# Inverse softmax sums of six of eight head pairs made inside a block's last pair; chain of the last two pairs beside the out-products

## The reference

```python
x = x + layernorm(attn(layernorm(x)))       # attn ends in: softmax(scores) @ v, heads joined, @ wo
x = x + layernorm(ffn(layernorm(x)))        # router, top 2 of 16 experts, one shared expert
```

## Time and profile before

| what | us |
|---|---|
| median of 3 runs | 1311.3 (1304.27 to 1312.95) |
| profiled execution, its own time | 1306.9 |
| its span, first to last instruction | 1305.1 |
| mean granted TensorE clock | 0.968 of full speed |
| PE busy | 1154.6 (88%) |
| DVE busy | 832.9 (64%) |
| ACT busy | 795.2 (61%) |
| POOL busy | 732.5 (56%) |

### The profile page before, as it was taken

The page is one execution under the profiler, slowest core; times in us unless marked ns, Lnnn a source line. Parts: engine busy times, 40 slices in busy tenths (PEclk is TensorE's granted clock), DMA queues, the critical chain, the costliest instruction groups (busy, mean ns, idle before and its releaser), DMA issues. The chain is left out here.

```text
span 1305.1 us, 19781 instructions
## 1 busy us (share of the span) xinstructions
PE 1154.6 (88%) x6552; PEld 549.4 (42%) x6563; DVE 832.9 (64%) x2104; ACT 795.2 (61%) x1237; POOL 732.5 (56%) x444
## 2 busy tenths in 40 slices
PE   3997999999998999999999979999999999788820
PEld 2643545344443533444443523333433334466710
DVE  6556786666667766565756786676666625745637
ACT  3633762766665466766666367777787783356632
POOL 0046541465564076766666248888888894435545
PEclk9988999999999999999999999999999999989975
DMA  9135300110011010000011001000000000367754
GB/s 286 34 87 131 91 1 1 49 33 17 21 45 34 6 44 17 17 17 17 17 33 32 11 13 57 26 13 13 25 25 25 13 13 17 71 130 211 187 135 141
DMA packets 63031, 70.25 MB, mean 54 GB/s; under 512 B 10080, under 2 KB 52448, under 8 KB 62816
## 3 DMA queue, kind: packets, MB, share of 16 engines
q1 hardware_dynamic: 56656, 56.26, 15.8%
q0 software_dynamic: 4864, 10.51, 3.7%
q10 hardware_dynamic: 1424, 2.38, 0.7%
HBM read 37.51 MB, written 14.83 MB: 40 GB/s over the span
## 5 line engine op out<-in xcount | busy, mean ns | idle before, releaser
L567 POOL TENSOR_TENSOR D<-D,B 128x1024 f32<-128x1024 f32 (+3 forms) x256 | 513.4, 2006 | 140.5 <-ACT B L759 120.2
L759 ACT ACTIVATE B<-ps 128x1024 f32<-128x1024 f32 (+1 forms) x320 | 285.2, 892 | 206.6 <-PE ps L1699 121.0
L1124 DVE TENSOR_REDUCE mxp<-ps 128x1 f32<-128x512 f32 x384 | 260.4, 688 | 177.2 <-PE ps L1673 175.1
L646 ACT ACTIVATE ps<-D 128x1024 f32<-128x1024 f32 (+3 forms) x327 | 288.3, 883 | 24.1 <-DVE D L1142 14.4
L1720 PE MATMUL ps<-B,kv 128*64 128x512 f32 (+3 forms) x1280 | 278.9, 545 | 0.3
L1699 PE MATMUL ps<-A,KTh 128*128 128x512 f16 (+3 forms) x768 | 209.0, 354 | 4.0 <-ACT ps L646 3.9
L560 POOL TENSOR_TENSOR D<-B 128x1024 f32<-128x1024 f32 (+1 forms) x32 | 70.8, 2213 | 209.1 <-ACT B L759 209.1
L1126 DVE CUSTOM_DVE_ANT_0 ps<-ps,c 128x128 f32<-128x128 f32 (+3 forms) x256 | 126.6, 496 | 76.9 <-PE ps L1673 73.4
L1673 PE MATMUL ps<-KTh,A 128*128 128x512 f16 (+3 forms) x384 | 134.4, 357 | 10.4 <-DVE mxp L1124 8.7
L1699 PE MATMUL ps<-A,KTl 128*128 128x512 f16 (+3 forms) x384 | 135.8, 354 | 0.0
L1720 PEld LDWEIGHTS ps<-B,kv 128*64 128x64 f32 x1280 | 73.6, 135 | 113.7 <-issue 97.0
(11 more groups left out here) (273 smaller groups left out, 1785.3 us busy)
## 6 DMA issues: line engine op xcount, KB each, us to landing
results<-B SPq DMA_DIRECT2D x64, 128.0 KB
xnTl<-in_L_ffn_experts_gate_up SPq DMA_DIRECT2D x16, 256.0 KB, 2.8
A<-in_L_attn_wq SPq DMA_DIRECT2D x4, 768.0 KB, 20.6
B<-in_L_attn_x SPq DMA_DIRECT2D x5, 512.0 KB, 5.6
D<-in_L_attn_wo SPq DMA_DIRECT2D x2, 1024.0 KB, 20.3
A<-C SPq DMA_DIRECT2D x16, 128.0 KB, 2.3
A<-C SPq DMA_DIRECT2D x32, 64.0 KB, 2.0
A<-stg SPq DMA_DIRECT2D x16, 128.0 KB, 2.3
```

The source lines that it names most:

```text
L567: nc.gpsimd.tensor_tensor(acc[:, :, c0:], acc[:, :, c0:], Pr[:, kt % P_RING, :, c0:], ALU.add).then_inc(sum_done, 1)
L646: return nc.scalar.activation(dst, src, ACT.Copy, scale=scale)
L759: nc.scalar.activation(Pr[:, kt % P_RING, :, c0:], ps[:, 2 * (kt % ST_RING):2 * (kt % ST_RING) + 2, c0:], ACT.Exp, scale=SM_SCALE).then_in ...
L1124: V.tensor_reduce(most, rough, AX.X, ALU.max).then_inc(mx_free, 1)
```

## The change

The denominators of pairs 0 to 5 are made inside the block's last pair (pair 7), at the slots of `EARLY`; those of pairs 6 and 7 (`LATE_PAIRS = 2`) after it. `Lp` is set to 1.0 at the kernel's start, so that the early reciprocal reads a number for the pairs that are not there yet; both chains work on all 16 heads. The terms, the turn and the copy are thus made twice in each block, with their own buffers (`early_terms` in `scr_r`, `early_rows` in `c32`). Inverse spreads go to banks 2 and 3 instead of 7 and 6.

At the block's end PE spreads pairs 0 and 1 at once, keeps four idle matmuls (before: 18, in block 3: 29), makes the products of row tiles 0 and 1 for pairs 0 to 5, then those of tile 2, among which the late chain's matmuls stand, then pairs 6 and 7 of tiles 0 to 2, and last the eight products of tile 3. DVE's layer-norm steps of the four tiles are staggered, with the moments of tiles 0 and 1 ahead of the first `with_input`.

```diff
+EARLY = [(3, 6), (18, 21), (24, 28), (6, 10)]
+LATE_PAIRS = 2
...
         def inv_bank(n):
-            return BK_O if n % 2 else BK_M
+            return 2 + n % 2
...
+                    if p == NP - 1 and kt == EARLY[qc][1] // 3:
+                        act.wait_ge(e_turned_ready, qc + 1)
+                        copy(early_rows[0:3 * H, :], ps[0:3 * H, BK_M, :]).then_inc(e_inv_ready, 1)
...
+                    if p == NP - 1 and slot == EARLY[qc][0] + 1:
+                        dve.wait_ge(e_den_ready, qc + 1)
+                        link(V.reciprocal(rL[:, :, :].rearrange("p h j -> p (h j)"), ps[:, BK_M, 0:H * TC]))
+                        terms(early_terms, early_rest, e_terms_ready)
...
+                for n in range(2):
+                    normalised(qc, n)
                 part_sums(qc, NP - 1)
+                for n in range(2, NP - LATE_PAIRS):
+                    normalised(qc, n)
...
+                for n in range(NP - LATE_PAIRS, NP):
                     normalised(qc, n)
+                if qc:
+                    choose(qc - 1, 3)
+
+                out_moments(qc, 0)
+                if qc:
+                    places(qc - 1, 1, 3)
+                out_moments(qc, 1)
+                with_input(qc, 0)
+                row_moments(qc, 0)
+                out_moments(qc, 2)
+                with_input(qc, 1)
+                row_scale(qc, 0)
+                row_moments(qc, 1)
+                out_moments(qc, 3)
+                with_input(qc, 2)
+                row_scale(qc, 1)
+                row_moments(qc, 2)
+                with_input(qc, 3)
+                row_scale(qc, 2)
+                row_moments(qc, 3)
...
+            def sums_of_parts(bank, ready):
+
+                parts = Lp[:, :, :].rearrange("p h (j b) -> p h j b", b=4)
+                for b in range(4):
+                    ins = T.matmul(ps[32 * b:32 * b + 32, bank, 0:H * TC], quads, parts[:, :, :, b],
+                                   start=True, stop=True)
+                ins.then_inc(ready, 1)
+
+            def turn_terms(terms, bank, ready):
+
+                for j in range(TC):
+                    ins = T.matmul(ps[0:3 * H, bank, j * P:(j + 1) * P],
+                                   terms[:, j, :, :].rearrange("p w h -> p (w h)"), identb,
+                                   start=True, stop=True)
+                ins.then_inc(ready, 1)
...
+                    if p == NP - 1 and slot == EARLY[qc][0]:
+
+                        pe.wait_ge(l_done, CR_L + qc * NP + NP - LATE_PAIRS)
+                        pe.wait_ge(wide_done, 2 * (nq * NP + np_) + int(Q_IN_LOOP(qc)))
+                        sums_of_parts(BK_M, e_den_ready)
+                    if p == NP - 1 and slot == EARLY[qc][1]:
+                        pe.wait_ge(e_terms_ready, qc + 1)
+                        turn_terms(early_terms, BK_M, e_turned_ready)
...
+                pe.wait_ge(e_inv_ready, qc + 1)
+                inv_spread(0)
+                inv_spread(1)
+                pe.wait_ge(mx_free, CR_MX + (first_unit(qc + 1) + units(qc + 1) if qc < NC - 1 else first_unit(NC)))
+                stay_busy(4, 1)
+                for n in range(NP - LATE_PAIRS):
+                    for j in range(2):
+                        out_product(j, n)
+                    if n + 2 < NP - LATE_PAIRS:
+                        inv_spread(n + 2)
+                    if n == 2:
+
+                        pe.wait_ge(l_done, CR_L + (qc + 1) * NP)
+                        sums_of_parts(0, den_ready)
...
+                for n in range(2):
+                    out_product(2, n)
+                pe.wait_ge(terms_ready, qc + 1)
+                turn_terms(inv_terms, 1, turned_ready)
+                for n in range(2, 4):
+                    out_product(2, n)
+                pe.wait_ge(inv_ready, qc + 1)
+                for n in range(NP - LATE_PAIRS, NP):
+                    inv_spread(n)
                 if qc < NC - 1:
                     prime(0)
...
+                for n in range(4, NP - LATE_PAIRS):
+                    out_product(2, n)
+                for j in range(3):
+                    for n in range(NP - LATE_PAIRS, NP):
+                        out_product(j, n)
                 if qc:
                     ranks(qc - 1, 3)
...
+                pe.wait_ge(o_free, CR_O + (qc + 1) * NP)
+                for n in range(NP):
+                    out_product(3, n)
                 if qc < NC - 1:
+                    if qc:
+                        pe.wait_ge(rank_read, qc)
+                    prime(1)
+                    pe.wait_ge(z_ready, qc * TC + 2)
```

More of the change, by code:

```diff
@@ L852, in _ @@
                     seed(qc + 1, 0, 0)
-                act.wait_ge(turned_ready, qc + 1)
-                copy(inv_rows[0:3 * H, :], ps[0:3 * H, BK_O, :]).then_inc(inv_ready, 1)
-                if qc < NC - 1:
[L857 to L866, removed]
+                    act.wait_ge(rows_out, 32 * qc)
+                root(qc, 0, 0)
+                root(qc, 1, 0)
+                root(qc, 0, 1)
+                root(qc, 2, 0)
+                normalised_rows(qc, 0)
+                if qc < NC - 1:
+                    act.wait_ge(primed, 2 * (qc + 1) + 2)
+                    seed(qc + 1, 0, 1)
+                root(qc, 1, 1)
+                root(qc, 3, 0)
+                normalised_rows(qc, 1)
+                root(qc, 2, 1)
             normalised_rows(NC - 1, TC - 2)
@@ L962, in _ @@
             link(V.memset(counts[:, 0, :], 0.0))
+            V.memset(Lp[:, :, :], 1.0)
             V.memset(expert_i[:, 0:NT], NE)
@@ L1365, in _ @@
                         choose(qc - 1, part)
-                for n in range(NP):
+                for n in range(NP - LATE_PAIRS, NP):
                     normalised(qc, n)
[L1368 to L1376, removed]
-                    row_moments(qc, j)
+                if qc:
[17 more added lines that the diff above has]
+                row_moments(qc, 3)
             row_scale(NC - 1, TC - 1)
@@ L1657, in prime, with stay_busy @@
                 ins.then_inc(primed, 1)
-            def stay_busy(times):
+            def stay_busy(times, bank=2):
                 for _ in range(times):
-                    T.matmul(ps[:, 2, :], zerob, c16[:, 0:CQ], start=True, stop=True)
+                    T.matmul(ps[:, bank, :], zerob, c16[:, 0:CQ], start=True, stop=True)
             def max_unit(qc, p, j):
@@ L1838, in _ @@
                     prime(0)
-                stay_busy(5 if qc < NC - 1 else 16)
-                pe.wait_ge(l_done, CR_L + (qc + 1) * NP)
-                pe.wait_ge(wide_done, min(2 * (qc + 1) * NP + 2, 2 * NC * NP))
-                parts = Lp[:, :, :].rearrange("p h (j b) -> p h j b", b=4)
-                for b in range(4):
-                    ins = T.matmul(ps[32 * b:32 * b + 32, BK_M, 0:H * TC], quads, parts[:, :, :, b],
-                                   start=True, stop=True)
-                ins.then_inc(den_ready, 1)
@@ L1847, in _ @@
-                pe.wait_ge(o_free, CR_O + (qc + 1) * NP)
-                stay_busy(10)
-                pe.wait_ge(terms_ready, qc + 1)
-                for j in range(TC):
-                    ins = T.matmul(ps[0:3 * H, BK_O, j * P:(j + 1) * P],
-                                   inv_terms[:, j, :, :].rearrange("p w h -> p (w h)"), identb,
-                                   start=True, stop=True)
-                ins.then_inc(turned_ready, 1)
-                stay_busy(3)
-                pe.wait_ge(inv_ready, qc + 1)
```

55 lines of the change are left out of this document (27 added, 28 removed).

## The result

The changed kernel takes 1322.8 us (median, 1321.9 to 1327.0) where the kernel before takes 1309.4 beside it: a ratio of 1.0112 with an interval of 1.0069 to 1.0154 (ratios here are taken over all runs, so they need not be the quotient of two medians). The forecast was 1310, in a range of 1298 to 1318. The profiled execution has a span of 1320.7, against 1305.1 before.

What follows compares the result with a forecast made beforehand. At block ends PE up to tile 0's products, then DVE, sets the pace. Losses of 7.0 less gains of 2.5 and 3.2 give +1.3 on 1306.9, so 1308.2, stated as 1310.0 us for a median; range 1298 to 1318.

Steps and rivals of the forecast that it cites:

- the first sentence on the early chain: Last pair of each block: the early chain adds 2.03 us on DVE, read from block 0's end before the change.
- The bounds of a pair: Loss in a last pair: 0.8 us if only PE's own work counts, up to 2.7; block 3 had 0 and 1.0.
- The step for block 3: Last pair of block 3: DVE idle, POOL the bound, PE's delay of about 1 mostly hidden; 0.5 us lost.
- +1.3: Whole kernel: 7.0 us lost in the last pairs, less gains of 2.5 and 3.2 at the block ends.
- The 0.8: Ends of blocks 0 to 2: each 0.8 us shorter, DVE's first maxima at T0 + 27.0 instead of T0 + 27.8.
- T0: Time of PE's last `values` at a block's end, 202.73 in block 0 before; tile 0's moments forecast at T0 + 15.1.
- Block 3's 3.2: End of block 3: 3.2 us gained, from 12.2 instead of 13.6 up to tile 0's moments and DVE's 11.7 instead of 13.5.
- PE's T0 + 20.6: Ends of blocks 0 to 2: PE is through its products at T0 + 20.6 against 24.3, then stands still.
- DVE and not PE releases the next block: Starts of blocks: PE's third `max_unit` waits for DVE; rival that PE releases: 0.11 at 1299.6, 0.07 at 1295 or less.
- The clock rival: Starts of blocks 1 to 3: idle PE falls to the lower clock, 1.5 to 3 us each; 1314 to 1318; chance 0.14.
- the 1.5 us to the first product: Block's end on PE: first product about 1.5 us after the last `values`, with no chain ahead of it.
- PE idle ahead of the turn in block 2: Last pairs: PE idle ahead of the early turn, about 1.2 us in block 2.

Runs made afterwards that it cites:

- the clock run: Against the changed kernel, operands in SBUF: PE runs 20 idle matmuls in block 2 and 25 in block 3 while waiting at the turn; 1323.9 us, ratio 1.0107.

## Why the prediction was wrong, step by step

**The step that failed** is the first sentence on the early chain: "It adds on DVE 2.03 (reciprocal and terms, 204.73 to 206.76)". The durations were right for a place where POOL stands still, and were carried to one where it adds. They are 2.8, 2.5, 5.5 and 7.8 there. The bounds of a pair, 0.8 and 2.7, took none of this row or all of it and nothing above it, so the range didn't see it either. The step for block 3 is the worst: "DVE is idle (9.0 us, rows above) and POOL the bound, so that PE's delay of about 1 is mostly hidden by POOL's backlog; 0.5 lost". It read POOL's 14 additions as cover and not as what holds DVE; 8.7 were lost, and POOL itself stood 8.15 us, since PE behind the turn gave it nothing to add.

That the rest of the sum was near is what the run with the operands in PSUM shows: with a chain of 2.3 us the pairs lose 2.9, 2.5, 2.4 and 0.4, against 2.5, 2.0, 2.0 and 0.5, the sum of pairs and ends is +0.3 against +1.3, and the time is 1310.9 against a stated 1310. Part of that is luck: the pairs lost 8.2 instead of 7.0 and the ends gave back 7.9 instead of 5.7, and the two misses are of opposite sign.

The Trainium skill ("SBUF — State Buffer", section "Who interferes with whom") has the rule that the prediction should have weighed: DVE instructions with two SBUF inputs, or copies and casts from SBUF to SBUF in a two-port mode, share a pair of ports with GpSimd, and the one that comes second is blocked for the whole instruction of the other. This case agrees: instructions that last up to 2.60 us beside additions of 2.4, and none held with an operand in PSUM; which mode a cast ran in the trace doesn't show. By that rule four instructions could each meet one addition of 2.4, an estimated 9.6 us; in the run with wider slots the four took 9.3.

**The ends.** The 0.8 was too small (2.2, 1.4, 1.1). In block 0 tile 0's moments came at T0 + 14.3, not 15.1, and DVE's part took 11.5, not 11.9, which the forecast had named as a sign that it is wrong. Block 3's 3.2 was counted from DVE's sum of pair 7, and from there it was 2.8 (28.6 to 25.8); the table's 3.4 is counted from the last exponential. Two sums are off by 0.1, three times 0.8 being 2.4 and PE's T0 + 20.6 adding up to 20.5; neither moves the forecast. That DVE and not PE releases the next block held: the third unit waits 2.68, 2.69 and 5.29 for it, where about 3, 3 and 5 were named.

**The clock rival** had its falls at the starts of blocks 2 and 3, 3.4 and 6.8 us at 0.50, but they cost nothing that can be seen: by the exponentials the kernel is 2.4 late at block 2's first and 2.4 at the start of its last pair, and over the same part of block 3 it loses 0.06. The prediction had 1.5 to 3 for each. The start of block 1 has no fall here; in three other executions that show 3.4 us at the lower level there with the layer norm in the same order (the clock run, the wider slots in SBUF, and the run with one operand put back), block 1 is 0.5 to 0.7 later by its last pair. The Trainium skill ("TensorE: Matmul & The Clock Gate", section "HAM oscillation — how this bites in real kernels") says that a wait between bursts lowers the clock. The rows agree at the starts of blocks 2 and 3 (waits of 2.69 and 5.29) and not at that of block 1 (2.68, no fall). What a fall costs may hang on who is late there; that was not tested. The falls that cost most, 2.0 and 2.8, lay behind the turns, where none was forecast.

**Told right:** the 1.5 us to the first product, PE idle ahead of the turn in block 2 as the place of the loss (4.54 instead of 1.2), and that the change loses more in the pairs than the ends of blocks 0 to 2 give back. Faster than before by over 1% was given 0.09, slower 0.05; the second should have been the larger.

## What to carry to other kernels

A duration belongs to the place it was read in: before a small DVE instruction is moved, look at what POOL does at the new place, and whether the instruction copies within SBUF or reads two operands there. If it does and POOL adds, put one operand in PSUM, which here cost 0.3 us over the chain (2.3 instead of 2.0) and saved 12 in all. And a wait in the order of PE delayed all that stood behind it (4.54 and 5.61 us at the turns, pairs 7.6 and 8.7 longer), so a chain that may be held wants room between its start and its reader; here that mended the pair of block 3, and not the time.

## What the hardware showed

- A held DVE instruction is shown as busy, with the hold in its duration: in block 3 1.76 to 2.60 us instead of 0.27 to 0.45, ending 0.1 to 0.3 after POOL's addition. The spread of a line's durations shows it; the waits don't.
- POOL starts its next addition 0.14 us after the last and ahead of the next linked DVE instruction (1066.80 against 1066.87), so that a chain pays what is left of an addition for each of its links: four of 1.76, 2.42, 2.50 and 2.60.
- A cast from PSUM takes 0.45 where one from SBUF takes 0.31; the subtraction takes 0.27 either way.
- A wait of 2.9 us was followed by a fall of the clock in one execution (6.8 us at the lower level, 2.8 us lost) and not in another of the same code; a wait of 1.43 likewise (6.8 us, 3.0 lost).
